# 16-head attention: the steps of a tile one slot closer together, and the maxima turned right behind the transposed scores

## The reference, cut to what matters

```python
q = (layernorm(x) @ Wq).reshape(b, -1, 16, 8).transpose(0, 2, 1, 3)
k = (ctx @ Wk).reshape(b, -1, 16, 8).transpose(0, 2, 1, 3)
v = (ctx @ Wv).reshape(b, -1, 16, 8).transpose(0, 2, 1, 3)
probs = softmax(einsum('bhqd,bhkd->bhqk', q, k) / sqrt(8), axis=-1)
attn = einsum('bhqk,bhkd->bhqd', probs, v)
x = x + attn.transpose(0, 2, 1, 3).reshape(b, -1, 128) @ Wo + bo
```

## Time and profile before

| | |
|---|---|
| median of three runs | 1642.81 us |
| profiled execution | 1629.38 us, span of its instructions 1627.5 us |
| PE / PEld busy | 1211.7 / 883.0 us (74% / 54%) |
| DVE / ACT / POOL busy | 1033.1 / 609.7 / 256.0 us |
| `largest` L654 | 96 times, 1217 ns |
| exponentials L560 | 96 times, 1020 ns |
| masked keys L605 | 48 times, 1899 ns |
| scores L449 | 384 matmuls, 356 ns |
| mean granted TensorE clock | 0.832 of full speed |

### The profile page before, as it was taken

The page is one execution under the profiler, slowest core; times in us unless marked ns, Lnnn a source line. Parts: engine busy times, 40 slices in busy tenths (PEclk is TensorE's granted clock), DMA queues, the critical chain, the costliest instruction groups (busy, mean ns, idle before and its releaser), DMA issues. The chain is left out here.

```text
span 1627.5 us, 22551 instructions
## 1 busy us (share of the span) xinstructions
PE 1211.7 (74%) x6771; PEld 883.0 (54%) x6805; DVE 1033.1 (63%) x3435; ACT 609.7 (37%) x1143; POOL 256.0 (16%) x240
## 2 busy tenths in 40 slices
PE   3688759999976655243916885999999999648852
PEld 1455549899964435221714553676777777335531
DVE  7577745666547886972356784555566655546868
ACT  3465124444432222111314652344444344336541
POOL 1232000001001100034365330000000000023302
PEclk8599879999995555565955996999999999968985
DMA  8442000000000013042224320000000000024301
GB/s 252 116 115 56 1 1 1 1 1 0 1 0 1 0 63 104 5 126 83 86 65 110 106 64 1 0 1 1 1 1 0 0 1 1 1 78 109 95 5 52
DMA packets 57700, 69.43 MB, mean 43 GB/s; under 512 B 10880, under 2 KB 38784, under 8 KB 56960
## 3 DMA queue, kind: packets, MB, share of 16 engines
q1 hardware_dynamic: 54272, 61.78, 13.3%
q0 software_dynamic: 3328, 6.43, 1.2%
HBM read 44.99 MB, written 23.59 MB: 42 GB/s over the span
## 5 line engine op out<-in xcount | busy, mean ns | idle before, releaser
L605 POOL TENSOR_TENSOR mha_ks<-KS,w_ctx 104x1024 fp32r<-104x1024 f32 (+1 forms) x48 | 91.0, 1899 | 698.3 <-POOLq L99 497.5
L2173 DVE SCALAR_TENSOR_TENSOR tree_hl<-tree_pH,tree_hh 128x512 fp32r<-128x512 f32 x192 | 132.3, 689 | 93.8 <-ACT tree_hh L2070 91.8
L2070 ACT ACTIVATE tree_hh<-tree_pH 128x512 fp32r<-128x512 f32 x192 | 114.6, 597 | 145.4 <-PE tree_pH L1974 111.4
L654 DVE TENSOR_REDUCE mha_nm<-mha_pS 128x16 f32<-128x1024 f32 x96 | 116.9, 1217 | 27.6 <-PE mha_pS L449 27.5
L449 PE MATMUL mha_pS<-mha_ks,mha_qs 96*128 96x256 f32 (+1 forms) x384 | 86.9, 356 | 47.2 <-DVE mha_nm L654 23.2
L1323 ACT ACTIVATE ffn_hid<-ffn_pH,w_ffn 128x512 f32<-128x512 f32 x128 | 85.3, 686 | 54.7 <-PE ffn_pH L1248 54.0
L1987 PE MATMUL tree_pY<-tree_hh,w2h 128*128 128x512 f32 x192 | 100.6, 524 | 4.7 <-DVE tree_hl L2173 4.4
L560 ACT ACTIVATE XH<-mha_pST 128x1024 f32<-128x1024 f32 x96 | 97.9, 1020 | 14.3 <-PE mha_pST L470 14.2
L449 PEld LDWEIGHTS mha_pS<-mha_ks,mha_qs 96*128 96x128 f32 (+1 forms) x384 | 63.1, 225 | 70.7 <-issue 39.1
L1432 DVE SCALAR_TENSOR_TENSOR ffn_acc<-ffn_pE,ffn_wt,ffn_acc 128x128 f32<-128x128 f32 x192 | 54.0, 343 | 71.2 <-PE ffn_pE L1261 71.2
L1261 PEld LDWEIGHTS ffn_pE<-W2R,ffn_hid 128*128 128x128 f32 x768 | 93.6, 192 | 4.4
(11 more groups left out here) (452 smaller groups left out, 2833.6 us busy)
## 6 DMA issues: line engine op xcount, KB each, us to landing
mha_qs<-queries SPq DMA_DIRECT2D x72, 256.0 KB, 4.1
queries<-mha_qh SPq DMA_DIRECT2D x24, 256.0 KB, 2.1
queries<-mha_ql SPq DMA_DIRECT2D x24, 256.0 KB, 2.5
EW<-in_L_W_dram SPq DMA_DIRECT2D x32, 128.0 KB, 2.8
EW<-in_tree_full_dram SPq DMA_DIRECT2D x2, 1536.0 KB, 8.2
slots_in<-route_zero SPq DMA_DIRECT2D x4, 640.0 KB, 11.6
w_rot<-in_rot_dram SPq DMA_DIRECT2D x1, 2307.0 KB, 8.3
X<-in_x_dram SPq DMA_DIRECT2D x8, 256.0 KB, 8.0
```

What stands on the lines that cost most here:

```text
L605: pool.tensor_tensor(ks[b % KB][0:K1, :, :, :], kb, hb, ALU.mult).then_inc(s["k"], 1)
L654: dve.tensor_reduce(nm[:, t, :], pS[:], AX.X, ALU.max, negate=True).then_inc(s["nm"], 1)
L2070: act.activation(hh[k % 2][:], pH[k % 2][:], ACT.Relu).then_inc(s["h"], 1)
L2173: dve.scalar_tensor_tensor(hl[k % 2][:], pH[k % 2][:], 0.0, hh[k % 2][:], ALU.max, ALU.subtract).then_inc(s["lo"], 1)
```

## The change

All steps from the transposed scores on come one slot closer to the scores: UN, AT, OE and HT each lose one, and the loop ends one slot earlier. On PE, `shifts` moves from behind `attend` to directly behind `scores_T`, ahead of `heads_T`. The test of ACT's `attended` now asks whether t-OE is even, since OE is odd. The first tile of a batch thereby meets `scores_T`, `attend`, `tokens` and `heads_T` in odd, odd, odd and even slots, where before these were even, even, even and odd; `shifts` and `split_shift` stay in even slots, and x_transposes, queries and their evacuations stay where they were.

```diff
-        FIRST, LAST = -8, T + 13
-        UN, AT, OE, HT = 6, 8, 10, 11
+        FIRST, LAST = -8, T + 12
+        UN, AT, OE, HT = 5, 7, 9, 10
...
                 if live(t - UN):
                     scores_T((t - UN) // TB, (t - UN) % TB)
+                if even(t) and live(t - 2):
+                    shifts((t - 2) // TB)
                 if live(t - HT):
                     heads_T(t - HT)
                 if live(t - AT):
                     attend((t - AT) // TB, (t - AT) % TB)
-                if even(t) and live(t - 2):
-                    shifts((t - 2) // TB)
...
-                if even(t) and live(t - OE):
+                if live(t - OE) and even(t - OE):
                     attended((t - OE) // TB)
```

## The result

The changed kernel takes 1619.83 us (median of four runs, 1618.83 to 1621.9), the kernel before 1640.82 us (1638.68 to 1644.06) on the same chip: ratio 0.9872, 95% interval 0.9849 to 0.9895. In a later comparison the same two kernels gave 0.9862 (0.9839 to 0.9885).

What follows compares the result with a forecast made beforehand. The prediction saw no single engine as the bound, but one PE standstill per slot of mha; -6.3 (end), -13.4 (keys), +1.5 (busy slot 10) and +7.6 (shifts) gave -10.6 us, scaled to 1632.1 us, range 1622 to 1645.

Steps and rivals of the forecast that it cites:

- the term of the keys: PE's scores in even slots no longer wait for GpSimd's keys: -13.4 us over three calls, at most about 19.
- One slot of the end, with the turn in it: End of each call: one slot of 2.11 us goes, -6.3 in three calls; slot 32 pays 0.23 for the earlier shifts.
- Shifts ahead of heads_T: PE's even slots: heads_T comes later behind shifts, 0.40 in slots 12 to 24, 0.23 in 26 to 32; +7.6 us.
- The rival in which the turn is free: PE's even slots: shifts cost nothing because PE fills its 0.52 us wait otherwise; -18.2 us, 1624.5 us, chance 0.19.
- The keys, as the waits in the rows: Steady slots: waits before the scores of 14, 18, 22 (0.33 each) and 26, 28, 30 (0.77 to 0.81) go; 3.0 + 7.1 us.
- The stretched VectorE work of the scales: Second call's filling: a small VectorE operation takes 0.83 us beside the keys, 0.17 with earlier keys; gain 0.66 us.
- The split of the maxima beside the keys: VectorE, steady stretch: L660 never above 0.2 after the change, named as a sign without a price.
- The filling: Slots 8 and 10: key waits go, 1.5 us in the first call, 1.1 in the third; heads_T and output cost 0.49 per call.
- From 1629.38 to the median in proportion: Whole kernel: forecast 1618.8 from the profiled 1629.38 us, scaled by the 0.82% higher median 1642.81, gives 1632.1 us.
- the waits go but not the time: PE's scores: another equally long wait stands behind GpSimd, only the end's slot is gained; 1645.6 us, chance 0.13.
- slower: Even slots pay more than odd ones give, as shifts wait for X behind a late output; 1649.5 us, chance 0.10.
- the read of the maxima lands late: Transposed scores wait for the DMA read, three slots after the turn instead of four; +4.8 us, 1637.0 us, chance 0.08.

Runs made afterwards that it cites:

- the distances alone: Kernel before with UN, AT, OE, HT one lower, the shorter loop and the new test of attended, shifts left behind attend: 1616.03 us, ratio 0.9848.
- five buffers: Kernel before with five key buffers instead of four in the third call alone, distances and order unchanged: 1638.58 us, ratio 0.9983.
- the two unused matmuls: Kernel before plus two 512-column matmuls, results unread, where PE waits for keys in slot 7 of first and third call: 1639.53 us, ratio 0.9992.

## Why the prediction was wrong

The sign was right, and the waits that were to go went; the step that failed is the size of the term of the keys, -13.4 us. In the 18 steady slots it measured 14.5 us for 10.1, since I priced a wait by the idle time in its row. In the fillings of the first and the third call the slots 7 to 11 lost 5.3 us for 1.6, in part since behind the wait the clock had fallen too, which had no term. Point by point:

- *One slot of the end, with the turn in it: -1.9 a call.* Right: from the last scores to the last `output` the calls lost 1.66, 2.05 and 1.90 us.
- *Shifts ahead of heads_T, +7.6.* Right, +7.2 when made alone, with 0.35 to 0.47 in the slots where 0.40 was foretold. The extra that was put at 0, in slots 14, 18, 22, is 0.09, and slots 15, 19, 23 lost 0.07. The rival in which the turn is free falls.
- *The keys, as the waits in the rows.* Too small by 0.25 each. I took the 0.33 us that the row names as idle. What the wait took from the slot is told by the starts: `output` 107.69 to scores 108.41 is 0.72 us, and the same pair unhindered in after is 104.47 to 104.61, 0.14. 0.72 - 0.14 = 0.58, and the slots lost just 0.58. The idle time counts from the end of the row of `output`, 107.69 + 0.39 = 108.08, while unhindered scores start long before that end. In the same way 0.77 and 0.81 were 1.01 and 1.07. Six slots in three calls by some 0.25: 4.4 us. All this stood in the trace of before: at the end of its slot 18 `output` starts at 111.54 and the scores 0.14 behind it:

```profile
111.68 0.72 PE L449 MATMUL mha_pS<-mha_ks,mha_qs 99*128 99x256 f32 x4
```

- *The stretched VectorE work of the scales, 0.7 in the second call.* The place was right and the size too small. I took 0.66 for one operation of 0.83 us; in that profile the next one, L745, took 0.56 as well. Which of them falls beside the keys differs from execution to execution. In the second profile of before:

```profile
905.53 1.86 DVE L745 TENSOR_TENSOR mha_nt<-mha_nt,RS 128x12 f32<-128x12 f32 x1
```

In after:

```profile
896.51 0.17 DVE L745 TENSOR_TENSOR mha_nt<-mha_nt,RS 128x12 f32<-128x12 f32 x1
```

In neither profile of after is one of L744 to L746 of that step above 0.17, and slots 8 and 9 of the second call take 7.98 us in both, for 9.10 and 9.77 before: 1.1 to 1.8. It is not safe: with the distances alone the keys fell on a cast of the maxima (1.78 us) there, and the two slots took 9.58.

- *The split of the maxima beside the keys.* The prediction named it as a sign (L660 never above 0.2 in the steady stretch; in after it is 0.12 to 0.18 from slot 12 on) but gave it no price, since in before it lies under the wait. Had only the wait gone, as with five buffers, 0.43 of each 0.58 would have been given back in the even slots.
- *The filling, 1.5 and 1.1 less 0.5 for a late slot 10.* Too small. From tile 7 to 12 the first and third call take 17.51 and 16.95 us in one profile of before, 17.53 and 17.50 in the other, and 14.58, 14.82, 14.78, 14.71 in the two of after: 2.65 in the mean, for 1.0 and 0.6. I put a price on the waits alone; the clock that falls behind the longest of them costs another 0.8 to 2 us a call, as the two unused matmuls showed (by tiles 7 to 12 or 8 to 12). The filling comes to 3.7 us over the two calls.
- *The second call.* It lost 6.4 us in the mean. Its filling scatters (44.8 and 48.8 us from tile 1 to 12 in the two profiles of before, 43.4 and 46.3 in those of after); in the mean it shrank by 2.0 us for the 0.2 foretold. The slots 8 and 9 above are most of that; the rest can't be put to a cause.
- *From 1629.38 to the median in proportion.* This did no harm: with the second span of before, 1640.4 and the 1.9 around it, the same sum gives 1631.7.

The keys' 4.4, the filling's 3.7 and the second call's 1.8 make 9.9 of the 10 us that the calls gained beyond the forecast (20.6 for 10.6).

Of the other rivals, *the waits go but not the time* is refuted by every odd slot, *slower* by the time, and *the read of the maxima lands late* by the rows of the transposed scores (L470): in the first profile of after none waits for a DMA, in the second a single one, 0.56 us at the end of the first call. One of the signs of being wrong did come, where the term had counted on it: in slot 8 of the first and the third call the scores wait for the maxima, 1.28 us, instead of for the keys.

On the rule of the Trainium skill ("TensorE: Matmul & The Clock Gate", section "Architectural detail: the array is 16x 32x32, not 1x 128x128") by which weight loads are pulled ahead: after the change the weights of `heads_T` load at 99.74, behind those of `shifts` at 99.60, which came 0.07 us after X was done. Here nothing passed a waiting instruction, and the 0.40 that I kept by the row was the better price.

## What to carry to other kernels

Price a wait by the distance between the starts of the two instructions around it, less the same distance where they meet unhindered; the idle time in a row was less here (0.33 for 0.58, 0.77 for 1.01). Look at what else runs under a wait before it is taken away: a second cost may lie there (the split stretched by the keys) and what starts when decides whether it comes out. Producing something earlier on one engine was worth nothing here while the engine that takes it on took it no earlier: moved on PE alone the turned maxima cost 7 us, and with one copy moved on ScalarE as well the even slots became up to 1 us shorter than in the changed kernel.

## What the runs showed of the hardware

VectorE's cast of 128x32 took 0.12 us alone and 0.76 while GpSimd multiplied the keys; its subtraction with both inputs in SBUF 0.19 and 0.57. The Trainium skill ("SBUF — State Buffer", section "Who interferes with whom") says that GpSimd and some VectorE operations take a shared pair of ports in turn, each for a whole instruction. The trace agrees in so far as the cast that started at 1550.97 ended at 1551.73, just behind the keys at 1551.69.

After PE had waited 2.23 us in the filling, the granted clock was 0.58 and 0.57 over the next 4 us; with matmuls in the wait it was 1.00 there. Behind a wait of 1.85 us for the maxima, with five buffers, it was 0.58 over the next slot; behind one of 1.28 us, in the kernel after, 1.00.

One stretch of unchanged code, from the routing to the experts, took 68.2 us in the first profile of before and 77.0 to 78.0 in the ten others of this study; why the first was short stays open.
